# Spreading the first two expert units of each batch over twelve lighter slots in a cross-attention schedule written out by hand

## The reference

```
x = LN(x + self_attention(x))            # 16 heads of 32, two attention products
x = LN(x + cross_attention(ctx, ctx, x)) # 16 heads of 32, softmax(QK/sqrt(512)) V, then Wo and bo
x = LN(x + moe(x))                       # below
moe: w = softmax(x @ gate_w)             # 8 experts, the two largest kept
     e0 = silu(x @ w0.T + b0); e1 = silu(x @ w1.T + b1)
     out = e0 * w[first] * (first is expert 0) + e1 * w[second] * (second is expert 1)
```

## Time and profile before

| | us |
|---|---|
| median of 3 runs | 1758.37 (1756.82 to 1758.61) |
| profiled execution, its time | 1754.45 |
| profiled execution, span of its instructions | 1752.7 |
| PE busy | 1663.1 (95%) |
| DVE busy | 1256.1 (72%) |
| POOL busy | 1160.6 (66%) |
| ACT busy | 992.1 (57%) |

### The profile page before, as it was taken

One profiled execution on the slowest core, in us unless ns is written; L12 is line 12 of the kernel. 1 busy time (PEld: TensorE's weight loads), 2 busy tenths in 40 slices (PEclk: granted clock), 3 DMA queues, 4 the chain that ended last, 5 costly groups with the idle time before them and its releaser, 6 DMA issues.

```text
span 1752.7 us, 30880 instructions
## 1 busy us (share of the span) xinstructions
PE 1663.1 (95%) x10584; PEld 1097.7 (63%) x10584; DVE 1256.1 (72%) x2786; ACT 992.1 (57%) x2002; POOL 1160.6 (66%) x963
## 2 busy tenths in 40 slices
PE   6999999999999889999998999999999999999998
PEld 4666666666666647877863456566565655656566
DVE  6677777777777656767876786877778687777845
ACT  4555555555555543433445666666666666667564
POOL 1555556556555564745565987969788786888874
PEclk9999999999999989999998999999999999999999
DMA  7566566565555555576625543535344344534210
GB/s 216 136 156 166 140 158 163 144 157 154 155 142 150 139 172 180 186 236 186 192 71 157 146 115 88 139 95 153 91 120 115 85 133 103 140 94 117 64 43 30
DMA packets 172311, 237.80 MB, mean 136 GB/s; under 512 B 22646, under 2 KB 74102, under 8 KB 172156
## 3 DMA queue, kind: packets, MB, share of 16 engines
q1 hardware_dynamic: 172156, 235.84, 49.0%
HBM read 92.10 MB, written 41.94 MB: 76 GB/s over the span
## 4 chain that ended last, share of the span: by engine, by line
PE 67%; DVE 12%; POOL 7%; DMA 5%; issue 3%; SPq 3%; ACT 2%; POOLq 0%; DVEq 0%; ACTq 0%
PE bank L1698 9%; POOL cross_added L2040 5%; PE bank L1567 5%; PE bank L203 5%; PE bank L204 5%; PE bank L1535 5%; PE bank L205 5%; DVE bank L620 5%; PE bank L1506 5%; PE bank L403 4%; PE bank L339 4%; PE bank L390 3%; SPq L752 2%; DVE bank L583 2%; PE bank L1603 2%
## 5 line engine op out<-in xcount | busy, mean ns | idle before, releaser
L1516 DVE TENSOR_REDUCE cross_negmax<-bank 128x1 f32<-128x512 f32 x512 | 338.8, 675 | 132.6 <-PE bank L1506 129.1
L1785 ACT ACTIVATE cpt<-bank 128x512 f32<-128x512 f32 x512 | 297.3, 595 | 122.6 <-PE bank L1535 119.9
L583 DVE CUSTOM_DVE_ANT_0 bank<-bank,future 128x128 f32<-128x128 f32 (+3 forms) x512 | 243.2, 488 | 172.2 <-PE bank L390 171.9
L465 ACT ACTIVATE pt<-bank 128x256 f32<-128x256 f32 (+3 forms) x512 | 217.7, 445 | 261.1 <-PE bank L339 254.9
L2040 POOL TENSOR_TENSOR cross_added<-cross_added,cpt 128x2048 f32<-128x2048 f32 x61 | 280.1, 4591 | 11.4 <-ACT cpt L1785 11.0
L652 POOL TENSOR_SCALAR_AFFINE_SELECT pt<-pt 128x512 f32<-128x512 f32 x128 | 81.1, 634 | 247.0 <-ACT pt L465 246.8
L1535 PE MATMUL bank<-cqk 98*128 98x512 f32 x512 | 225.8, 441 | 10.0 <-ACT cpt L1785 9.5
L1506 PE MATMUL bank<-cqk 96*128 96x512 f32 x512 | 211.6, 417 | 11.0 <-DVE cross_negmax L1516 8.9
L2040 POOL TENSOR_TENSOR cross_added<-cpt,cpt 128x2048 f32<-128x2048 f32 x32 | 146.7, 4585 | 78.1 <-ACT cpt L1785 78.1
L339 PE MATMUL bank<-qk 98*128 98x256 f32 (+2 forms) x512 | 179.2, 355 | 10.5 <-ACT pt L465 4.9
L390 PE MATMUL bank<-qk 96*128 96x256 f32 (+2 forms) x512 | 169.1, 336 | 5.5 <-DVE self_negmax L583 4.4
(11 more groups left out here) (210 smaller groups left out, 3619.9 us busy)
## 6 DMA issues: line engine op xcount, KB each, us to landing
qk<-stage SPq DMA_DIRECT2D x384, 128.0 KB, 2.4
cqk<-cstage SPq DMA_DIRECT2D x384, 128.0 KB, 2.3
scratch_memory<-memory SPq DMA_DIRECT2D x64, 256.0 KB, 3.8
ma<-scratch_memory SPq DMA_DIRECT2D x32, 512.0 KB, 4.0
raw<-in_x_t SPq DMA_DIRECT2D x32, 256.0 KB, 2.9
v<-in_x SPq DMA_DIRECT2D x32, 256.0 KB, 3.3
scratch_y_ar<-y_ar SPq DMA_DIRECT2D x32, 256.0 KB, 2.7
my_ar<-scratch_y_ar SPq DMA_DIRECT2D x32, 256.0 KB, 4.5
```

The lines of the kernel that those rows point to most:

```text
L583: dve.tensor_tensor_reduce(out=scores, in0=scores, in1=sh.future[:, SEQ - P * (qt + 1):SEQ], scale=-1.0, scalar=-NEG, op0=ALU.add, op1=ALU ...
L1516: dve.reduce_max(s.negmax[gm % 2][:, col:col + 1], max_bank(sh, m)[:, :], AX, negate=True).then_inc(s.dve_max, 1)
L1785: act.activation(s.pt[step % 3][:, j, :], sh.bank[2 + n % 2][:, :], ACT.Exp, scale=SCALE_CROSS).then_inc(s.act_exp, 1)
```

## The change

Units 0 and 1 of each batch get six slots each instead of three, with two products in a slot (one ahead of L1506, one at the end): unit 0 in slots 30 to 35, unit 1 in slots 41 to 46. Units 2 to 7 keep four products a slot and three slots each, from slot 47, so that every one starts three slots sooner and the last ends in slot 64. What follows a unit (tanh, silu, weighing, join, statistics, factors, application, store) moves three slots sooner with it; for unit 0 tanh moves from slot 47 to 36 and silu from 48 to 37. The gate's products move from bank 6 to bank 7, where its scratch is, since unit 0 is in bank 6 at that time; unit 1 is in bank 6 too, and from unit 2 on even units are in bank 7 and odd ones in bank 6. Of a batch's transpositions the first now goes to bank 6 and the other three to bank 7; the fourth moves from slot 33 to 34 and its low part from 35 to 36. Two units have their bias by a product, as before (now units 0 and 2); ACT writes the others'.

```diff
-ADD, FACTORS, APPLY, TRANSPOSE = (16, 17, 21, 25), (18, 19, 23, 27), (20, 22, 26, 30), (24, 27, 31, 33)
-LOW = (29, 30, 33, 35)
-GATE, LOGITS, EXPERT = 37, 42, 44
+ADD, FACTORS, APPLY, TRANSPOSE = (16, 17, 21, 25), (18, 19, 23, 27), (20, 22, 26, 30), (24, 27, 31, 34)
+LOW = (29, 30, 33, 36)
+GATE, LOGITS = 37, 42
-STATS3, FACTORS3, APPLY3, STORE = (58, 64, 68, 76), (59, 65, 69, 78), (66, 71, 73, 81), (67, 72, 74, 82)
-UNITS, UNIT_SLOTS = 2 * TILES, 3
+STATS3, FACTORS3, APPLY3, STORE = (55, 61, 65, 73), (56, 62, 66, 75), (63, 68, 70, 78), (64, 69, 71, 79)
+UNITS = 2 * TILES
+UNIT = (30, 41, 47, 50, 53, 56, 59, 62)
+UNIT_SLOTS = (6, 6, 3, 3, 3, 3, 3, 3)
+PREFILL = {1: 39, 3: 49, 4: 52, 5: 55, 6: 58, 7: 61}
+TANH = (36, 47, 50, 53, 56, 59, 62, 65)
+SILU = (37, 48, 51, 54, 57, 60, 63, 66)
+WEIGH = (46, 49, 52, 55, 58, 61, 64, 67)
+JOIN = (47, 50, 53, 56, 59, 62, 65, 68)
+def unit_bank(sh, u):
+    return sh.bank[7 if u >= 2 and u % 2 == 0 else 6]
+def x2t_bank(sh, k):
+    return sh.bank[6 if k == 0 else 7]
...
                 if b >= 1:
-                    pe.wait_ge(s.dve_u, UNITS * b - 1 + k)
+                    pe.wait_ge(s.dve_u, UNITS * b - k)
...
-            pe.wait_ge(s.dve_x2t, TILES * b + k - 1)
+            pe.wait_ge(s.dve_x2t, TILES * b + k)
...
-        if u == 0:
-            pe.wait_ge(s.act_lt, b + 1)
-            if b == 0:
-                pe.wait_ge(s.pool_exp_lo, 2 * GROUPS)
-        elif u == 1:
+        if u == 0:
+            pe.wait_ge(s.dve_x2t, TILES * b + 1)
+        elif u == 2:
             pe.wait_ge(s.dve_gate, GATE_OPS * (b + 1))
...
-    for part in range(4 * third + 2 * half, 4 * third + 2 * half + 2):
+    some = 3 * GROUPS // (2 * UNIT_SLOTS[u])
+    for part in range(some * (2 * at + half), some * (2 * at + half) + some):
```

More of the change, by code:

```diff
@@ L1648, in cross_batch @@
         else:
-            pe.wait_ge(s.dve_x2t, TILES * b + k - 1)
+            pe.wait_ge(s.dve_x2t, TILES * b + k)
         for c in range(GROUPS):
-            done = pe.transpose(sh.bank[6 + k % 2][:, tile_of(c)], s.x2[:, k, tile_of(c)], sh.ident[:, :])
+            done = pe.transpose(x2t_bank(sh, k)[:, tile_of(c)], s.x2[:, k, tile_of(c)], sh.ident[:, :])
         done.then_inc(s.pe_x2t, 1)
@@ L1655, in cross_batch @@
         pe.wait_ge(s.dve_x2t, TILES * (b + 1))
-        done = triple(pe, sh.bank[6][0:EXPERTS, :], (cw.gate_hi[:, c, :], cw.gate_lo[:, c, :]),
+        done = triple(pe, sh.bank[7][0:EXPERTS, :], (cw.gate_hi[:, c, :], cw.gate_lo[:, c, :]),
                       (s.x2t_hi[:, c, :], s.x2t_lo[:, c, :]), c == 0, c == GROUPS - 1)
@@ L1676, in cross_expert @@
 def cross_expert(pe, s, cw, sh, b, slot, half):
-    if not EXPERT <= slot < EXPERT + UNITS * UNIT_SLOTS:
+    u = max((unit for unit in range(UNITS) if UNIT[unit] <= slot), default=None)
+    if u is None or slot >= UNIT[u] + UNIT_SLOTS[u]:
         return
-    u, third = divmod(slot - EXPERT, UNIT_SLOTS)
     k, i = divmod(u, 2)
-    bank = sh.bank[6 + u % 2]
-    if third == 0 and half == 0:
+    bank, at = unit_bank(sh, u), slot - UNIT[u]
+    if at == 0 and half == 0:
         if u == 0:
-            pe.wait_ge(s.act_lt, b + 1)
-            if b == 0:
-                pe.wait_ge(s.pool_exp_lo, 2 * GROUPS)
-        elif u == 1:
+            pe.wait_ge(s.dve_x2t, TILES * b + 1)
+        elif u == 2:
             pe.wait_ge(s.dve_gate, GATE_OPS * (b + 1))
@@ L1691, in cross_expert @@
             pe.wait_ge(s.act_bias, bias_written(b, u))
-        if u < 2:
+        if b == 0 and u < 2:
+            pe.wait_ge(s.pool_exp_lo, 2 * GROUPS - 1 + u)
+        if u not in PREFILL:
             cross_bias(pe, cw, bank, 1 + i)
-    for part in range(4 * third + 2 * half, 4 * third + 2 * half + 2):
+    some = 3 * GROUPS // (2 * UNIT_SLOTS[u])
+    for part in range(some * (2 * at + half), some * (2 * at + half) + some):
         c, which = divmod(part, 3)
@@ L1698, in cross_expert @@
         done = pe.matmul(bank[:, :], x[:, c, tile_of(k)], w[:, i, c, :], start=False, stop=(part == 11),
-                         skip_group_check=(u >= 2))
-    if third == UNIT_SLOTS - 1 and half == 1:
+                         skip_group_check=(u in PREFILL))
+    if at == UNIT_SLOTS[u] - 1 and half == 1:
         done.then_inc(s.pe_ex, 1)
@@ L1796, in cross_batch_scalar @@
             act.wait_ge(s.pe_ex, UNITS * b)
-        x2t_high(act, s, sh.bank[6 + k % 2], b, k)
+        x2t_high(act, s, x2t_bank(sh, k), b, k)
     if slot == LOGITS - 1:
@@ L1803, in cross_batch_scalar @@
         act.wait_ge(s.pe_q, min(GROUPS * (b + 1) + LOGITS // SLOTS + 3, NG))
-        act.activation(s.x1t[0:EXPERTS, :], sh.bank[6][0:EXPERTS, :], ACT.Copy).then_inc(s.act_lt, 1)
+        act.activation(s.x1t[0:EXPERTS, :], sh.bank[7][0:EXPERTS, :], ACT.Copy).then_inc(s.act_lt, 1)
     if slot == LOGITS + 2:
@@ L1807, in cross_batch_scalar @@
         act.activation(gate_scratch(sh.bank[7], 1), s.ge[:, :, :], ACT.Exp).then_inc(s.act_gate, 1)
[L1808 to L1812, removed]
+    for u in PREFILL:
+        if slot == PREFILL[u]:
+            cross_bias_written(act, s, cw, sh, b, u)
+    if slot in TANH:
+        u = TANH.index(slot)
         act.wait_ge(s.pe_ex, UNITS * b + u + 1)
@@ L1815, in cross_batch_scalar @@
             act.wait_ge(s.pool_x2, UNITS * b + u - 1)
-        act.activation(s.tanh[u % 2][:, :], sh.bank[6 + u % 2][:, :], ACT.Tanh, scale=0.5).then_inc(s.act_tanh, 1)
-    if r == 2 and 0 <= u < UNITS:
+        act.activation(s.tanh[u % 2][:, :], unit_bank(sh, u)[:, :], ACT.Tanh, scale=0.5).then_inc(s.act_tanh, 1)
+    if slot in WEIGH:
+        u = WEIGH.index(slot)
         k, i = divmod(u, 2)
@@ L1827, in bias_written @@
 def bias_written(b, u):
-    return 9 * b + 3 * (u // 2 - 1) + (1, 3)[u % 2]
+    return 10 * b + {1: 2, 3: 4, 4: 5, 5: 7, 6: 8, 7: 10}[u]
 def cross_bias_written(act, s, cw, sh, b, u):
-    bank = sh.bank[6 + u % 2]
-    act.wait_ge(s.dve_u, UNITS * b + u - 1)
+    bank = unit_bank(sh, u)
+    act.wait_ge(s.dve_u, UNITS * b + (1 if u == 1 else u - 1))
     if u % 2 == 0:
@@ L1910, in cross_batch_vector @@
         k = LOW.index(slot)
-        x2t_low(dve, s, sh.bank[6 + k % 2], b, k)
+        x2t_low(dve, s, x2t_bank(sh, k), b, k)
     if slot == LOGITS + 1:
@@ L1916, in cross_batch_vector @@
         cross_gate_weights(dve, s, sh.bank[7], b, UNITS * b)
-    u, r = divmod(slot - EXPERT - UNIT_SLOTS - 1, UNIT_SLOTS)
-    if r == 0 and 0 <= u < UNITS:
+    if slot in SILU:
+        u = SILU.index(slot)
         tanh = s.tanh[u % 2]
         dve.wait_ge(s.act_tanh, UNITS * b + u + 1)
-        dve.scalar_tensor_tensor(out=tanh[:, :], in0=tanh[:, :], scalar=1.0, in1=sh.bank[6 + u % 2][:, :],
+        dve.scalar_tensor_tensor(out=tanh[:, :], in0=tanh[:, :], scalar=1.0, in1=unit_bank(sh, u)[:, :],
                                  op0=ALU.add, op1=ALU.mult).then_inc(s.dve_u, 1)
@@ L2001, in cross_slot_gpsimd @@
             s.ln2.factors(pool, b, FACTORS.index(slot))
-        u, r = divmod(slot - EXPERT - 2 * UNIT_SLOTS, UNIT_SLOTS)
-        if r == 0 and 0 <= u < UNITS:
+        if slot in JOIN:
+            u = JOIN.index(slot)
             x = s.x2[:, u // 2, :]
@@ L2217, in tail_gate, with tail_bank @@
     done.then_inc(s.pe_gate, 1)
+def tail_bank(sh, u):
+    return sh.bank[7 - u % 2]
 def tail_expert(pe, s, cw, sh, u):
     k, i = divmod(u, 2)
-    bank = sh.bank[6 + u % 2]
+    bank = tail_bank(sh, u)
     pe.wait_ge(s.dve_u, UNITS * LAST_BATCH + u - 1)
@@ L2265, in tail_tanh @@
     act.wait_ge(s.pool_x2, n - 1)
-    act.activation(s.tanh[u % 2][:, :], sh.bank[6 + u % 2][:, :], ACT.Tanh, scale=0.5).then_inc(s.act_tanh, 1)
+    act.activation(s.tanh[u % 2][:, :], tail_bank(sh, u)[:, :], ACT.Tanh, scale=0.5).then_inc(s.act_tanh, 1)
 def tail_weigh(act, s, u):
@@ L2309, in tail_silu @@
     dve.wait_ge(s.act_tanh, UNITS * LAST_BATCH + u + 1)
-    dve.scalar_tensor_tensor(out=tanh[:, :], in0=tanh[:, :], scalar=1.0, in1=sh.bank[6 + u % 2][:, :],
+    dve.scalar_tensor_tensor(out=tanh[:, :], in0=tanh[:, :], scalar=1.0, in1=tail_bank(sh, u)[:, :],
                              op0=ALU.add, op1=ALU.mult).then_inc(s.dve_u, 1)
```

## The result

The changed kernel takes 1769.24 us (median of 7 runs, 1762.80 to 1773.05) against 1759.16 us of the kernel before (7 runs, 1756.82 to 1767.62). The ratio is 1.0044 with a 95% interval of 1.0024 to 1.0065: slower by 4 to 11 us (the two medians lie 10.1 us apart), where 1755.6 with a range up to 1763.5 was predicted. The profiled execution took 1770.64 us; its span is 1768.9.

A forecast was written before the change was run, and what follows sets the result against it. PE bounds the kernel, POOL nearly level in a batch's first half. A, B and C give +1.2 us seven times, D -1.3 six times, E -3.4: together -2.8, from 1758.4 to 1755.6 us, range 1746.5 to 1763.5.

The forecast's parts named there:

- A: Slots 30 to 35: 12 products and a bias added, 3.03 us, less 1.6 of room; +1.4 us a batch.
- B: Slots 41 to 43: six products added at 0.233 us each; +1.4 us a batch.
- C: Slots 44 to 46: seven products fewer on a full PE; -1.63 us a batch.
- D: Slots 65 to 67: 12 products fewer, gain limited by POOL's third addition; -1.3 us between batches, six times.
- the rival that all products hide there: Slots 30 to 36: POOL sets PE's arrival, all 13 products hide; total -12.6 us, 1745.8 us; chance 0.14.
- the slow rival on the release of bank 6: Slot 68: bias product waits for a late silu, gain there is 0; total +5.0 us, 1763.4 us; chance 0.14.
- the fast rival on POOL: Slot 68: POOL's third addition does not hold PE back, full 2.8 us gained; total -11.8, 1746.6 us; chance 0.14.
- E: After the last batch's slots: 12 products (2.8 us) and a silu (0.67) leave the chain; -3.4 us once.
- New waits around unit 0: Last three transpositions share bank 7 and may stall PE; total +0.7 to +4.2 us, up to 1762.6; chance 0.13.

The follow-up runs named there:

- the two repairs: Changed kernel with the third tile's factors in slot 67, behind the low part: 1760.56 us; with second and third tiles' factors in slots 67 and 69: 1755.70 us.

## Why the prediction was wrong

The change was forecast at -2.8 us and is +7.7 by the ratio (4.2 to 11.4); the part that the trace shows in the cross phase is +5.6. Parts A to D came out by the mechanism that was given for them; the miss is an instruction that was in none of them.

*A, slots 30 to 36: right.* +1.4 forecast, +1.21 measured; 10.64 us from slot 30 to the sum against 10.8. The room, read as 1.6 us from three gaps, was 3.03 - 1.21 = 1.8, and the rival that all products hide there is refuted: of their 3.03 us only 1.8 were hidden, though POOL was busy throughout the window. The sum no longer waits for POOL once PE is later.

*B and C: right.* +1.39 against +1.40 and -1.70 against -1.63. The price of 0.233 us for a matmul holds in both signs. By the figure of the Trainium skill ("TensorE: Matmul & The Clock Gate", section "Wait — 56ns, not 53.3ns?", 0.2157 us) the six products of B would cost 1.29. The trace has 1.39, and it decides.

*D, slots 65 to 68: right as far as it went, and here is the step that failed.* -1.09 against -1.3. The silu released the bias product 1309.15 - 1306.54 = 2.6 us after the start of slot 65, exactly at its forecast place, so the slow rival on the release of bank 6 fell. The third addition held the sum back by 0.43 us, where 1.8 - 1.35 = 0.45 was forecast, so the fast rival on POOL fell too. Then the text says: "After it POOL has a join and a factor set less before its next addition at 1302.63, so it stays level with PE up to slot 20." That is true of the addition, and false of what lies between. The low part of y stands in that queue (in a stretch of the earlier trace rows that is left out there), and slot 70's projection reads it. Before the change it ended 1.2 us before PE wanted it. Of the kernel before, first the set of factors behind the third addition's join and the low part in POOL's timeline, then slot 70's start and its projection in PE's:

```profile
1295.95 0.22 POOL L187 TENSOR_SCALAR ln_rstd<-ln_mv 128x1 f32<-128x1 f32 x1
...
1297.37 1.27 POOL L2029 TENSOR_TENSOR cy_lo<-cross_y_raw,cy_hi 128x512 fp32r<-128x512 f32 x1
```

```profile
1299.59 0.40 PE L1535 MATMUL bank<-cqk 98*128 98x512 f32 x1
1299.83 0.40 PE L1671 MATMUL bank<-wo_hi,cy_hi 128*128 128x512 f32 x1
```

The low part's end at 1298.64 leaves 1.19 us to the projection. The change made it about 1.4 us later, measured from slot 55 (the additional set ahead of the third addition), and PE about 1.1 us earlier, and 2.5 of shift less 1.2 of slack is 1.3 us of waiting. In the profile the projection stands 1315.92 - 1314.27 = 1.65 us behind the start of the slot and not 0.24, and 0.1 more is lost in the first matmul after the wait: 1.5 in all. The prediction named who waits behind the addition, and put the rest of POOL's queue at nothing, though one instruction in it has a reader on PE. With this term (six times 1.5 = +9) the sum -2.8 becomes +6.2, and the trace shows +5.6.

*E, the end: right mechanism, size off.* -3.4 forecast; the tail shrank from 62.8 to 60.6 us in the first profiles, -2.2, and lies between 60.4 and 62.2 in the profiles of kernels that have the change's tail. Half of what is missing may be the wait for a low part of y in the tail, which is 2.06 us now and was 1.45; this was not tested.

*New waits around unit 0.* The rival has no part in the result: the slots 30 to 35 are the same in the kernel with unit 0 alone, and that one is the fastest. The transposition of slot 27 does wait 0.5 us or more for DVE in all seven batches of the changed kernel. It does so too in the kernel before with the late low part, where no unit is moved, but in only one or two batches of the two repairs, so it goes with the late low part. It costs nothing: slots 26 and 27 are 0.35 us longer, slots 21 and 22 as much shorter.

**What is shown and what is not.** That the wait for the low part of y costs what the change lost is shown twice, by taking it away from the changed kernel and by adding it to the kernel before. That slot 70 is long because of POOL's order and not because of PE's load is shown too. Not settled is a rest of 2 to 4 us that lies outside the slots. The changed kernel's cross phase is 5.6 us longer and its runs are 7.7 and 8.6 us slower, with intervals that reach down to 4.2 and 5.6. Its two repairs show the same: their cross phases take 1.2 and 6.9 us less than the mean of the two of the kernel before, but their runs are 1.1 us more and 3.2 less. The kernel before with the late low part has 1.8 us of such a rest, the one with unit 0 alone none. The cross phase starts later in the five profiles of kernels with moved products (898 to 905 us against 892 to 900 in the other three), though the code ahead of it is the same. Part of that is clock (last section); whether any of it belongs to the kernel stays open. With the missing term the forecast would have been 1758.4 + 6.2 = 1764.6 us. The measured 1769.24 is 4.6 above it; 0.8 of this is the kernel before, now at 1759.16, and the other 3.8 are for the most part this rest.

## What to carry to other kernels

When work is taken out of a saturated stretch, list every instruction in the other engines' queues that falls due in it, with the time between its end and its reader, and not only the long one that the wait row names: here an instruction of 1.3 us with 1.2 us of slack cost 1.5 us a batch, about as much as each of the parts that were worked out (1.1 to 1.7). If an engine issues in order, adding a short set of operations ahead of such an instruction is a change to its reader. And of a change that moves several things, try the part with the best ratio alone: moving unit 0 into a stretch with room, and spreading unit 1 over the slots that it leaves, brought 10 us; going on to shift all the others took it away again, and 7 us of it even with POOL's order mended.

## What the runs showed of the hardware

The granted clock of PE differs from execution to execution in places where the code is the same. The windows view of the changed kernel (busy us of PE, PEld, DVE, ACT, POOL, each with its count, then clock, DMA share and rate) has one such place in its second batch:

```profile
1033.90:1040.70 6.80, 6.43 (x20) 3.14 (x20) 4.51 (x10) 3.53 (x7) 6.47 (x7) 0.50 0.01 2
```

That is the lower of the clock's two levels (1.2 GHz) for 6.8 us, and matmuls in it stand 0.43 us apart and not 0.233. It follows on a wait of PE of 1.71 us, before which the clock was granted in full. The wait alone does not settle it: at the same place the second profile of the kernel before has a wait of 1.79 us and the granted clock 0.50 from 1026.4 to 1033.2 us, while the unaltered repeat of the changed kernel has a wait of 1.84 us and a clock of 1.00 throughout (1024 to 1038 us). That is 104.87 us for this batch against 101.37 in the repeat. The mean clock is 0.982 over this span and 0.985 to 0.990 in the others, and the busy time of PE goes with it: 1670.3 us here, 1659.9 to 1668.1 in the others, for the same 10584 matmuls.

The start of the cross phase moves as well. It is the first matmul of the phase in each of the two profiles of the kernel before:

```profile
892.29 0.50 PE L1535 MATMUL bank<-cqk 98*128 98x512 f32 x1
```

```profile
895.83 0.50 PE L1535 MATMUL bank<-cqk 98*128 98x512 f32 x1
```

In the changed kernel it is 902.89. Of the 16.2 us between the two profiled spans 10.6 lie ahead of the phase that the diff touches. The clock can account for most of them: from 600 to 680 us it was 0.83 against 0.91 in the first profile of the kernel before, and from 780 to 850 us 0.95 against 1.00. As an estimate from these figures, 80 x 0.08 + 70 x 0.05 = 9.9 us at most. Two single executions would have told a story of 16 us. The slot times are what repeats, to 0.02 us in most slots, and the medians of many runs are what the change is worth.
